# Second norm on ScalarE, one convolution tap and the sum on VectorE, and the norm shifts on POOL in the fuse phase of a ViT, memory and MoE kernel on one Trainium2 core

## The chip, the cores and the metric

One core of one Trainium2 chip runs the whole program in one launch. The metric is the time of the program on the device in microseconds (us). "Engines" are TensorE (PE in the rows, its weight loads PEld), VectorE (DVE), ScalarE (ACT), GpSimd (POOL) and SyncE (SP, which here only issues DMAs).

## The reference, cut to what matters

The model is a small vision transformer over 64 images (196 patches and a class token, 128 wide, 4 layers), then a memory block over 197 + 32 text tokens for each image, then a mixture of experts. The changed phase stands between the transformer and the memory block. It computes this:

```python
h = layernorm(h, norm_w, norm_b)                   # first norm: last step of the transformer
h = jnp.concatenate([h, txt], axis=1)              # 197 + 32 = 229 tokens
z = _layernorm(h)                                  # second norm: (h - mean) / sqrt(var + eps)
xc = conv1d_depthwise(z, conv_w, taps=4, padding=(3, 0)) + conv_b[:, None]
eta_mean   = sigmoid(xc + gelu(xc @ eta_w1) @ eta_w2).mean(axis=(0, 2))
alpha_mean = sigmoid(xc + gelu(xc @ alpha_w1) @ alpha_w2).mean(axis=(0, 2))
```

Each output token of the convolution is, channel by channel, a weighted sum of its own token and the three before it; tap 3 is the token's own. `xc` is kept for the memory block, and the two means become the decay and the drift of the memory.

## The kernel before

The program is a row of phases with a barrier behind each: `layers_phase` (the transformer), `fuse_phase` (the changed one), `gate_phase` (means and scans), `memory_phase` and `tail_phase` (routing and experts). `fuse_phase` works on pairs of images: 32 pairs, 458 tokens each (`WL`). A pair lies as four tiles of 99 or 98 tokens (token on the partition, 128 channels along the row) and a fifth with the 2 x 32 text tokens.

Each engine runs its own loop over an index `i`, unrolled, in the order in which its code is written, and does a different stage of a different pair in each pass: a software pipeline. Semaphores (`f_...`) tie the engines, and an engine does not go past a wait. The stages of pair `n` are, in this order:

- First norm, for pairs from 6 on (the first six were normed in the layers phase): `first_stats` and `first_aggr` (mean and variance into `mv`), `first_rstd` on POOL (`ve` = variance + eps, then `rstd` by a power of -0.5), `first_shift` on VectorE (-mean x rstd), `normalise` on ScalarE (x * rstd + shift into `y`), `weight` on VectorE and `bias` on POOL. SP then writes `y` to memory as `hcat`.
- Second norm: `second_stats` and `second_aggr` on VectorE, `second_rstd` on POOL, `scale` on VectorE: `z` = y x rstd. The mean is not taken off here. Instead the four diagonal matrices of the convolution are multiplied once, ahead of the loop, by (identity - 1/128), into `diag`.
- `turn` on TensorE: five transposes into the bank `f_T`, with the image tokens of both images first and the text tokens behind them. `turned_out` on ScalarE copies the bank into `zT` in two instructions, so that each image's 229 tokens stand in a row behind three zero columns.
- `conv` on TensorE: four matmuls, one for each tap, added up in the bank `f_C`. `conv_out` on ScalarE adds the bias and writes `xc`, a slice of `xT`.
- `up` on TensorE, `gelu` on ScalarE, `down` on TensorE, `argument` on VectorE (adds `xc`), `tanh` on ScalarE (the sigmoid), `sums` on POOL: twice each, for eta and alpha.

Around the middle of the phase one pass of a loop does `down(i-2)`, `conv(i+1)`, `turn(i+2)`, `up(i)` on TensorE, and `sums(i-3)`, `second_rstd(i+4)`, `bias(i+5)`, `first_rstd(i+7)` on POOL. `memory_phase`, which the change leaves alone, has a norm whose steps are laid out as those of the changed kernel are: variance + eps and -mean on VectorE (L1573, L1574), power and shift on POOL (L1520, L1523).

Of the kernel before, what the change touches and what calls it, by code (L numbers as in the profile page):

```python
# [977 lines left out]
def fuse_phase(nc, g, A):  # L978

    LAST = 7  # L980
    with ExitStack() as ctx:
        s = Sems(nc, ctx, "f_taps f_gate_w f_txt f_set f_diag f_centred "
                 + " ".join(f"f_txt{p} f_out{p}" for p in range(4)) +
                 " f_stats f_aggr f_ve f_rstd f_shift f_xn f_xw f_y f_stats2 f_aggr2 f_ve2 f_rstd2 "
                 "f_z f_turned f_zT f_conv f_xc f_up f_gelu f_down f_arg f_tanh f_sum")

        def sb(name, shape, dt=F32):
# [5 lines left out]
        mv, ve, rstd, shift = ([sb(f"{n}{p}", [TC, 4, w]) for p in range(2)]
                               for n, w in (("mv", 2), ("ve", 1), ("rstd", 1), ("shift", 1)))
        mv2, ve2 = sb("mv2", [TC, 5, 2]), sb("ve2", [TC, 5, 1])
        rstd2 = [sb(f"rstd2{p}", [TC, 5, 1]) for p in range(2)]
# [18 lines left out]
        with nc.Block() as block:  # L1015
# [1192 lines left out]
```

## Time and profile before

| what | value |
|---|---|
| median of 3 runs | 3659.69 us (3652.66 to 3664.78) |
| the profiled execution's own time | 3660.88 us |
| its span | 3659.1 us |
| mean granted TensorE clock | 0.975 of full speed |
| fuse phase, first instruction to barrier | about 2600 to 2850 us of the span |
| busy over the span | PE 3379.4, DVE 2384.5, POOL 2279.2, ACT 2018.8 us |

The whole program is listed by engine in the profile, but the changed phase is only 7% of it. So the busy shares of the span say little here, and the rows further down come from views that are cut to that phase: busy time by stretch, instructions in order of time, and the minimum, median and maximum duration of one line's instructions.

### The profile page before, as it was taken

What the parts mean: (1) busy time and instruction counts of PE and PEld (TensorE: products, weight loads), DVE (VectorE), ACT (ScalarE), POOL (GpSimd) and SP (SyncE); (2) the same over time, 40 slices, a digit from 0 to 9 for tenths busy, and PEclk for the clock granted to TensorE, in tenths of its full rate; (3) what the DMA queues carried; (4) which work ended last, traced back from release to release, by engine and by line L of the source; (5) the groups of instructions that cost most, each with busy time, mean ns of one, the idle gap of its engine ahead of it and who ended that gap; (6) DMA issues with size and microseconds to landing.
All of it is one profiled execution on the core that took longest, in us unless ns stands there. A gap on an engine that the chain in (4) does not pass through costs nothing. (4 is left out here: it accounts for less than half of the span.)

```text
span 3659.1 us, 87958 instructions
## 1 busy us (share of the span) xinstructions
PE 3379.4 (92%) x29756; PEld 2580.2 (71%) x29756; DVE 2384.5 (65%) x6229; ACT 2018.8 (55%) x3948; POOL 2279.2 (62%) x2634
## 2 busy tenths in 40 slices
PE   7999999989999899999999999999899898999983
PEld 4577787777787677777777777777544686766762
DVE  2267777657777666777766677766698677885110
ACT  0156666656666665666665666667465464323331
POOL 0356664576666386666548666637598684377886
PEclk9999999999999999999999999999999899999997
DMA  6856675046766315766703666640111133143443
GB/s 221 271 110 127 127 132 104 9 84 127 132 129 127 60 28 105 129 127 127 131 12 61 123 128 127 130 82 1 39 33 27 54 83 58 35 105 74 68 62 32
DMA packets 456073, 342.26 MB, mean 94 GB/s; under 512 B 70659, under 2 KB 440171, under 8 KB 455595
## 3 DMA queue, kind: packets, MB, share of 16 engines
q1 hardware_dynamic: 404419, 275.69, 38.9%
q10 hardware_dynamic: 24224, 46.44, 3.9%
q0 software_dynamic: 27136, 16.42, 3.4%
q8 instruction: 159, 2.61, 0.3%
q14 instruction: 135, 1.11, 0.1%
HBM read 227.68 MB, written 109.29 MB: 92 GB/s over the span
## 5 line engine op out<-in xcount | busy, mean ns | idle before, releaser
L795 DVE TENSOR_REDUCE a_neg_max<-a_S 99x4 f32<-99x788 f32 x1024 | 1003.7, 980 | 484.9 <-PE a_S L346 481.3
L558 ACT ACTIVATE a_shared<-a_St 99x792 f32<-99x792 f32 (+1 forms) x1024 | 851.2, 831 | 637.2 <-PE a_St L363 626.0
L363 PE MATMUL a_St<-a_q_st,a_k_st 99*99 99x198 bf16 (+1 forms) x4096 | 527.8, 251 | 55.4 <-DMA a_q_st<-a_max_rows 39.1
L346 PE MATMUL a_S<-a_k_st,a_q_st 96*99 96x197 bf16 x4096 | 538.7, 254 | 39.4 <-DVE a_neg_max L795 39.4
L346 PEld LDWEIGHTS a_S<-a_k_st,a_q_st 96*99 96x99 bf16 x4096 | 390.0, 126 | 255.0 <-DVE a_neg_max L795 216.8
L382 PE MATMUL a_O<-a_shared,a_v_aug 99*32 99x198 f32 (+1 forms) x8192 | 464.8, 339 | 0.4
L363 PEld LDWEIGHTS a_St<-a_q_st,a_k_st 99*99 99x99 bf16 (+1 forms) x4096 | 390.3, 126 | 84.9 <-DMA a_q_st<-a_max_rows 48.1
L707 POOL CAST a_parts<-a_q_k 128x792 bf16<-128x792 f32 x128 | 107.8, 842 | 321.3 <-issue 281.2
L382 PEld LDWEIGHTS a_O<-a_shared,a_v_aug 99*32 99x32 f32 (+1 forms) x8192 | 247.0, 110 | 84.3 <-issue 1.8
L687 POOL CAST a_max_parts<-a_neg_max 99x32 bf16<-99x32 f32 x128 | 26.8, 210 | 406.7 <-DVE a_neg_max L795 406.7
L498 PEld LDWEIGHTS a_O<-a_w,a_shared 128*99 128x99 f32 x2048 | 243.2, 167 | 40.8 <-issue 23.1
L498 PE MATMUL a_O<-a_w,a_shared 128*99 128x128 f32 x2048 | 265.6, 273 | 0.9 <-DVE h L892 0.9
L1934 POOL DMA_INDIRECT out<-h,token x128 | 210.1, 1641 | 53.7 <-issue 36.3
L627 ACT ACTIVATE a_shared<-a_St,a_cols 128x396 f32<-128x396 f32 x256 | 148.7, 590 | 152.1 <-PE a_St L509 144.5
L709 POOL TENSOR_TENSOR a_q_k<-a_q_k,a_parts 128x792 f32<-128x792 f32 x128 | 216.2, 1689 | 10.3
L715 POOL TENSOR_TENSOR a_parts<-a_q_k,a_parts 128x792 bf16<-128x792 f32 x128 | 215.7, 1685 | 10.3
L509 PE MATMUL a_St<-a_shared,a_w 128*128 128x396 f32 x512 | 196.2, 506 | 0.0
L723 POOL TENSOR_TENSOR h<-h,a_rows 99x512 f32<-99x512 f32 x128 | 162.9, 1273 | 34.8 <-ACT a_shared L634 34.8
L1878 ACT ACTIVATE z_gel<-z_U,z_sb 128x458 f32<-128x458 f32 x128 | 81.9, 644 | 174.0 <-PE z_U L1756 165.1
L1878 ACT ACTIVATE z_gel<-z_U,z_eb 128x458 f32<-128x458 f32 x128 | 82.4, 644 | 165.0 <-PE z_U L1756 153.2
L1981 DVE TENSOR_TENSOR h<-z_O,xT 120x512 f32<-120x512 f32 x32 | 22.1, 690 | 225.3 <-DMA out<-h,token 176.6
L634 ACT ACTIVATE a_shared<-h,a_m_rstd 99x128 f32<-99x128 f32 x512 | 162.1, 390 | 3.2 <-POOL a_m_rstd L734 3.2
(271 smaller groups left out, 7312.4 us busy)
## 6 DMA issues: line engine op xcount, KB each, us to landing
a_shared<-in_x ACTq DMA_DIRECT2D x64, 594.0 KB, 5.0
spill_q<-a_parts SPq DMA_DIRECT2D x384, 99.0 KB
spill_k<-a_parts SPq DMA_DIRECT2D x384, 99.0 KB
a_k_st<-spill_k SPq DMA_DIRECT2D x128, 297.0 KB, 4.0
a_q_st<-spill_q SPq DMA_DIRECT2D x128, 297.0 KB, 6.2
a_k_st<-spill_k SPq DMA_DIRECT2D x128, 198.0 KB, 4.6
a_q_st<-spill_q SPq DMA_DIRECT2D x128, 198.0 KB, 6.7
a_k_st<-spill_k SPq DMA_DIRECT2D x128, 99.0 KB, 4.9
```

What stands on the lines that cost most here:

```text
L346: mm = nc.tensor.matmul(S[0:TC, j // 2, j % 2 * TB:j % 2 * TB + NTOK], q_st[p % 4][0:SPLIT, head, b * TB + c * TC:b * TB + (c + 1) * TC], ...
L363: mm = nc.tensor.matmul(St[0:keys, j // 2, j % 2 * TB:(j % 2 + 1) * TB], k_st[p][:, head, first:first + keys], q_st[p][:, head, b * TB:(b ...
L382: mm = nc.tensor.matmul(O[32 * j:32 * j + 32, half * TB:(half + 1) * TB], v_aug[p % 4][0:keys, 2 * b + c, half * 4 + j, :], probs[0:keys, ...
L498: mm = nc.tensor.matmul(O[0:TC, t * D:(t + 1) * D], gl[k % 2][:, h, t * TC:(t + 1) * TC], m.w2[:, h * D:(h + 1) * D], start=(h == 0), stop ...
L509: nc.tensor.matmul(St[:, h, 0:PW], m.w1[:, h * 128:(h + 1) * 128], m_yT[n % 2], start=True, stop=True).then_inc(s["m_fc1"], 1)
L558: nc.scalar.activation(probs[0:keys, u % 4, :].rearrange("p (x t) -> p x t", x=2), St[0:keys, :, 0:2 * TB], ACT.Exp).then_inc(s["probs"], 1)
L709: nc.gpsimd.tensor_tensor(q_k[:], q_k[:], parts[:, 0, :, :], ALU.subtract).then_inc(s["res"], 1)
L715: nc.gpsimd.tensor_tensor(parts[:, 2, :, :], q_k[:], parts[:, 1, :, :], ALU.subtract).then_inc(s["lo"], 1)
L723: nc.gpsimd.tensor_tensor(hp, hp, m.b2.unsqueeze(1).to_broadcast([TC, 4, D]), ALU.add).then_inc(s["m_bias"], 1)
L795: nc.vector.tensor_reduce(out.rearrange("p (x y) -> p x y", x=2), S[0:TC, :, 0:2 * TB].rearrange("p x (y t) -> p x y t", y=2)[:, :, :, 0:N ...
L1878: nc.scalar.activation(gel[n % 2][:, k, 0:WL], U[k][:, 0:WL], ACT.Gelu_apprx_tanh, bias=bias).then_inc(s["gelu"], 1)
L1934: nc.gpsimd.indirect_dma_start(out=out[:, :], out_offset=bass.IndirectOffsetOnAxis(g.token[0:n, e, k:k + 1].bitcast(U32), 0), in_=y[(2 * e ...
```

## The change

Five parts, all in `fuse_phase`:

1. ScalarE computes the second norm in full: `normalise_again` makes `z` = y x rstd + shift, in five instructions of 99 x 128, as `normalise` does for the first norm. VectorE's `scale` goes, and so do the matmul and the copy that centred the diagonal matrices.
2. Both shifts are made on POOL, behind the power (-mean x rstd, 99 x 4 or 99 x 5). The small additions of eps, until now on POOL, and the -mean are done by VectorE right behind each `bn_aggr`, on tiles of 4 or 5 columns. VectorE's `first_shift` goes.
3. The convolution keeps taps 0 to 2 on TensorE. Tap 3 with the bias is `first_part` on VectorE: it reads the turned rows in PSUM and writes `xc`. `conv_sum` on VectorE adds the bank `f_C` to it. ScalarE's `conv_out` goes, and `turn` waits for `first_part` too.
4. `turn` writes the text rows to their final place (its fifth transpose writes 2 x 32 columns), so that ScalarE's `turned_out` is one copy of 458 columns.
5. The order of the loops differs: on ScalarE `gelu`, `normalise`, `tanh`, `normalise_again`, `turned_out`; on VectorE `first_part` leads and `conv_sum` ends, with both `argument` in the middle; on POOL `first_rstd` is moved from the end of a pass, for pair i+7, to the head of the next pass, for pair i+6.

```diff
                 def conv(n):
...
-                    for k in range(4):
+                    for k in range(3):
...
                 def turn(n):
                     wait(pe, s["f_z"], n + 1)
                     wait(pe, s["f_zT"], n)
+                    wait(pe, s["f_first"], n)
...
-                def conv_out(n):
-                    wait(act, s["f_conv"], n + 1)
-                    nc.scalar.activation(xc(n), Cp[:, 0:WL], ACT.Identity, bias=taps[:, 4:5]).then_inc(s["f_xc"], 1)
+                def normalise_again(n):
+                    wait(act, s["f_shift2"], n + 1)
+                    wait(act, s["f_turned"], n - 1)
+                    for t in range(5):
+                        a = nc.scalar.activation(z[n % 2][:, t, :], normed(n, t), ACT.Identity,
+                                                 bias=shift2[n % 2][:, t, :], scale=rstd2[n % 2][:, t, :])
+                    a.then_inc(s["f_z"], 1)
...
-                    nc.scalar.activation(zT[n % 2][:, :, 3:3 + NTOK],
-                                         Tp[:, 0:2 * NTOK].rearrange("p (b l) -> p b l", b=2), ACT.Copy)
-                    nc.scalar.activation(zT[n % 2][:, :, 3 + NTOK:],
-                                         Tp[:, 2 * NTOK:WL].rearrange("p (b l) -> p b l", b=2),
+                    nc.scalar.activation(zT[n % 2][:, :, 3:], Tp[:, 0:WL].rearrange("p (b l) -> p b l", b=2),
                                          ACT.Copy).then_inc(s["f_zT"], 1)
...
                 def second_rstd(n):
-                    wait(pool, s["f_aggr2"], n + 1)
-                    wait(pool, s["f_rstd2"], n)
-                    nc.gpsimd.tensor_tensor(ve2[:, :, 0], mv2[:, :, 1], g.eps[0:TC, 0:1].to_broadcast([TC, 5]),
-                                            ALU.add).then_inc(s["f_ve2"], 1)
-                    wait(pool, s["f_ve2"], n + 1)
+                    wait(pool, s["f_ve2"], 2 * (n + 1))
                     wait(pool, s["f_z"], n - 1)
-                    nc.gpsimd.tensor_tensor(rstd2[n % 2][:, :, 0], ve2[:, :, 0],
+                    nc.gpsimd.tensor_tensor(rstd2[n % 2][:, :, 0], ve2[n % 2][:, :, 0],
                                             g.neg_half[0:TC, 0:1].to_broadcast([TC, 5]),
                                             ALU.pow).then_inc(s["f_rstd2"], 1)
+                    wait(pool, s["f_rstd2"], n + 1)
+                    nc.gpsimd.tensor_tensor(shift2[n % 2][:, :, 0], nm2[n % 2][:, :, 0], rstd2[n % 2][:, :, 0],
+                                            ALU.mult).then_inc(s["f_shift2"], 1)
...
-                def scale(n):
-                    wait(dve, s["f_rstd2"], n + 1)
-                    wait(dve, s["f_turned"], n - 1)
...
+                def first_part(n):
...
+                    wait(dve, s["f_zT"], n + 1)
+                    nc.vector.tensor_scalar(xc(n), Tp[:, 0:WL], taps[:, 3:4], taps[:, 4:5], ALU.mult,
+                                            ALU.add).then_inc(s["f_first"], 1)
+
+                def conv_sum(n):
+                    wait(dve, s["f_conv"], n + 1)
+                    wait(dve, s["f_first"], n + 1)
+                    nc.vector.tensor_tensor(xc(n), Cp[:, 0:WL], xc(n), ALU.add).then_inc(s["f_xc"], 1)
...
                 def second_aggr(n):
...
+                    wait(dve, s["f_aggr2"], n + 1)
+                    wait(dve, s["f_shift2"], n - 1)
+                    nc.vector.tensor_scalar(ve2[n % 2][:, :, 0], mv2[:, :, 1], EPS, None, ALU.add).then_inc(s["f_ve2"], 1)
+                    nc.vector.tensor_scalar(nm2[n % 2][:, :, 0], mv2[:, :, 0], -1.0, None, ALU.mult).then_inc(s["f_ve2"], 1)
```

The first norm's `first_rstd` and `first_aggr` are changed as the second norm's are, with 4 columns for 5.

On VectorE, one pass of the middle of the phase is these rows in the kernel before (`f_z<-f_y` is `scale`, `f_shift` is `first_shift`, `f_arg` is `argument`, `f_mv` is one of the two `bn_aggr`):

```order
L1199 TENSOR_TENSOR f_z<-f_y,f_rstd 99x640
L1210 BN_STATS f_stats<-f_y 99x6 x5
L1230 SCALAR_TENSOR_TENSOR f_shift<-f_mv,f_rstd 99x4
L1236 BN_STATS f_stats<-h 99x6 x4
L1217 BN_AGGR f_mv<-f_stats 99x2 x5
L1222 TENSOR_TENSOR f_y<-f_y,norm 99x512
L1249 TENSOR_TENSOR f_arg<-f_Z,xT 128x458
L1243 BN_AGGR f_mv<-f_stats 99x2 x4
L1249 TENSOR_TENSOR f_arg<-f_Z,xT 128x458
```

and these in the changed one:

```order
L1191 TENSOR_SCALAR xT<-f_T,f_taps 128x458
L1206 BN_STATS f_stats<-f_y 99x6 x5
L1213 BN_AGGR f_mv<-f_stats 99x2 x5
L1217 TENSOR_SCALAR f_ve<-f_mv 99x5
L1218 TENSOR_SCALAR f_nm<-f_mv 99x5
L1247 TENSOR_TENSOR f_arg<-f_Z,xT 128x458 x2
L1222 TENSOR_TENSOR f_y<-f_y,norm 99x512
L1229 BN_STATS f_stats<-h 99x6 x4
L1237 BN_AGGR f_mv<-f_stats 99x2 x4
L1241 TENSOR_SCALAR f_ve<-f_mv 99x4
L1242 TENSOR_SCALAR f_nm<-f_mv 99x4
L1197 TENSOR_TENSOR xT<-f_C,xT 128x458
```

The two instructions with two inputs in SBUF that led to `z` and to the shift are out; two that read PSUM and four of 4 or 5 columns are in, and each `bn_aggr` now stands right behind its statistics. On POOL, one pass was this (`gate_sum` is `sums`):

```order
L1146 TENSOR_TENSOR gate_sum<-gate_sum,f_arg 128x458 x2
L1152 TENSOR_TENSOR f_ve<-f_mv,eps 99x5
L1156 TENSOR_TENSOR f_rstd<-f_ve,neg_half 99x5
L1162 TENSOR_TENSOR f_y<-f_y,norm 99x512
L1170 TENSOR_TENSOR f_ve<-f_mv,eps 99x4
L1174 TENSOR_TENSOR f_rstd<-f_ve,neg_half 99x4
```

and is now this:

```order
L1166 TENSOR_TENSOR f_rstd<-f_ve,neg_half 99x4
L1170 TENSOR_TENSOR f_shift<-f_nm,f_rstd 99x4
L1143 TENSOR_TENSOR gate_sum<-gate_sum,f_arg 128x458 x2
L1149 TENSOR_TENSOR f_rstd<-f_ve,neg_half 99x5
L1153 TENSOR_TENSOR f_shift<-f_nm,f_rstd 99x5
L1158 TENSOR_TENSOR f_y<-f_y,norm 99x512
```

The two additions of eps are gone from POOL, a product stands behind each power, and the first norm's power leads the pass.

## Rows read from the trace of the kernel before

**Rows 1.** Busy us (xcount) of PE, PEld, DVE, ACT, POOL in a stretch; PEclk.

```profile
2640.00:2740.00 100.00, 99.34 (x297) 48.34 (x295) 97.04 (x317) 62.56 (x153) 93.76 (x97) 1.00 0.13 34
```

**Rows 2.** `conv_out` by itself in three stretches: count, first to last start.

```profile
L1109 ACT ACTIVATE xT<-f_C,f_taps x7: 622/642/644, 2619.8 to 2659.9; 128x458 f32<-128x458 f32 x7
...
L1109 ACT ACTIVATE xT<-f_C,f_taps x21: 619/623/625, 2659.9 to 2805.1; 128x458 f32<-128x458 f32 x21
...
L1109 ACT ACTIVATE xT<-f_C,f_taps x6: 625/642/643, 2805.1 to 2838.6; 128x458 f32<-128x458 f32 x6
```

**Rows 3.** Timeline, middle of the phase: start, us, engine, line, [idle before].

```profile
2741.19 1.27 POOL L1162 TENSOR_TENSOR f_y<-f_y,norm 99x512 f32<-99x512 f32 x1
2741.25 1.88 DVE L1199 TENSOR_TENSOR f_z<-f_y,f_rstd 99x640 f32<-99x640 f32 x1
...
2743.06 1.05 DVE L1210 BATCH_NORM_STATS2 f_stats<-f_y 99x6 f32<-99x128 f32 x5
...
2744.27 2.10 POOL L1146 TENSOR_TENSOR gate_sum<-gate_sum,f_arg 128x458 f32<-128x458 f32 x2
2744.33 1.13 DVE L1230 SCALAR_TENSOR_TENSOR f_shift<-f_mv,f_rstd 99x4 f32<-99x4 f32 x1 [0.21 <-POOL f_rstd L1174]
...
2745.50 1.65 ACT L1103 ACTIVATE f_y<-h,f_shift,f_rstd 99x128 f32<-99x128 f32 x4 [2.73 <-DVE f_shift L1230]
...
2746.16 0.42 DVE L1217 BATCH_NORM_AGGREGATE f_mv<-f_stats 99x2 f32<-99x6 f32 x5
...
2747.08 0.62 DVE L1249 TENSOR_TENSOR f_arg<-f_Z,xT 128x458 f32<-128x458 f32 x1
...
2747.82 0.30 PEld L1046 LDWEIGHTS f_Z<-f_gel,f_gate_w 128*128 128x128 f32 x2 [0.79 <-issue]
```

**Rows 4.** Timeline, end of the phase: PE's weight loads at `down` and `conv`.

```profile
2819.61 0.19 PEld L1046 LDWEIGHTS f_Z<-f_gel,f_gate_w 128*128 128x128 f32 x1 [0.19 <-issue]
...
2826.51 0.19 PEld L1046 LDWEIGHTS f_Z<-f_gel,f_gate_w 128*128 128x128 f32 x1 [0.19 <-issue]
...
2830.35 0.19 PEld L1055 LDWEIGHTS f_C<-f_zT,f_diag 128*128 128x128 f32 x1 [0.20 <-issue]
2830.73 0.19 PEld L1055 LDWEIGHTS f_C<-f_zT,f_diag 128*128 128x128 f32 x1 [0.20 <-issue]
```

**Rows 5.** Single lines: duration in ns, minimum/median/maximum.

```profile
L1230 DVE SCALAR_TENSOR_TENSOR f_shift<-f_mv,f_rstd x26: 139/1132/1137, 2625.7 to 2802.4; 99x4 f32<-99x4 f32 x26
...
L1156 POOL TENSOR_TENSOR f_rstd<-f_ve,neg_half x32: 1164/1176/1285, 2610.3 to 2818.5; 99x5 f32<-99x5 f32 x32
```

**Rows 6.** Timeline of the memory phase, where the same small steps stand already.

```profile
2886.38 1.27 POOL L1506 TENSOR_TENSOR y_hc<-y_hc,y_qn 115x512 f32<-115x512 f32 x1
...
2886.89 0.79 DVE L1573 TENSOR_SCALAR y_ve<-y_mv 115x4 f32<-115x4 f32 x1
...
2955.82 0.55 ACT L1478 ACTIVATE xT<-y_ZT 128x458 f32<-128x458 f32 x1
2955.88 0.17 DVE L1573 TENSOR_SCALAR y_ve<-y_mv 115x4 f32<-115x4 f32 x1
2955.95 0.16 DVE L1574 TENSOR_SCALAR y_nm<-y_mv 115x4 f32<-115x4 f32 x1
...
2956.20 1.02 POOL L1520 TENSOR_TENSOR y_rstd<-y_ve,neg_half 115x4 f32<-115x4 f32 x1 [0.81 <-DVE y_nm L1574]
...
2957.29 0.20 POOL L1523 TENSOR_TENSOR y_shift<-y_nm,y_rstd 115x4 f32<-115x4 f32 x1
```

**Rows 7.** Timeline, start of the phase: a power on POOL beside VectorE.

```profile
2624.13 1.35 POOL L1174 TENSOR_TENSOR f_rstd<-f_ve,neg_half 99x4 f32<-99x4 f32 x1
...
2624.52 0.29 DVE L1199 TENSOR_TENSOR f_z<-f_y,f_rstd 99x128 f32<-99x128 f32 x1
```

**Rows 8.** Timeline, late in the phase: `scale` beside `sums`.

```profile
2806.34 3.96 DVE L1199 TENSOR_TENSOR f_z<-f_y,f_rstd 99x640 f32<-99x640 f32 x1 [0.26 <-POOL f_rstd L1156]
...
2807.51 2.10 POOL L1146 TENSOR_TENSOR gate_sum<-gate_sum,f_arg 128x458 f32<-128x458 f32 x2
```

More of the change, by code:

```diff
@@ L990, in fuse_phase @@
         taps, gate_w, norm = sb("taps", [D, 5]), sb("gate_w", [D, 4, D]), g.norm
-        centre, tap_diag, diag = sb("centre", [D, D]), sb("tap_diag", [D, 4, D]), sb("diag", [D, 4, D])
+        diag = sb("diag", [D, 3, D])
         stats, stats2 = sb("stats", [TC, 4, 6]), sb("stats2", [TC, 5, 6])
[L993 to L996, printed above, removed]
+        mv, mv2 = sb("mv", [TC, 4, 2]), sb("mv2", [TC, 5, 2])
+        ve, nm, rstd, shift = ([sb(f"{n}{p}", [TC, 4, 1]) for p in range(2)] for n in ("ve", "nm", "rstd", "shift"))
+        ve2, nm2, rstd2, shift2 = ([sb(f"{n}2{p}", [TC, 5, 1]) for p in range(2)] for n in ("ve", "nm", "rstd", "shift"))
         y = [sb(f"y{p}", [TC, 5, D]) for p in range(4)]
@@ L1132, in _ @@
                         normalise(i + 6)
-                    if live(i + 1):
-                        conv_out(i + 1)
+                    if live(i - 2):
+                        tanh(i - 2)
+                    if live(i + 3):
+                        normalise_again(i + 3)
                     if live(i + 2):
                         turned_out(i + 2)
-                    if live(i - 2):
-                        tanh(i - 2)
             @block.gpsimd
@@ L1167, in first_rstd @@
                     p = n % 2
-                    wait(pool, s["f_aggr"], n + 1 - NORMED)
-                    wait(pool, s["f_rstd"], n - 1 - NORMED)
-                    nc.gpsimd.tensor_tensor(ve[p][:, :, 0], mv[p][:, :, 1], g.eps[0:TC, 0:1].to_broadcast([TC, 4]),
-                                            ALU.add).then_inc(s["f_ve"], 1)
-                    wait(pool, s["f_ve"], n + 1 - NORMED)
+                    wait(pool, s["f_ve"], 2 * (n + 1 - NORMED))
                     wait(pool, s["f_xn"], n - 1 - NORMED)
@@ L1176, in first_rstd @@
                                             ALU.pow).then_inc(s["f_rstd"], 1)
+                    wait(pool, s["f_rstd"], n + 1 - NORMED)
+                    nc.gpsimd.tensor_tensor(shift[p][:, :, 0], nm[p][:, :, 0], rstd[p][:, :, 0],
+                                            ALU.mult).then_inc(s["f_shift"], 1)
                 nc.gpsimd.memset(g.gate_sum[:], 0.0).then_inc(s["f_set"], 1)
@@ L1256, in _ @@
                     if i == 4 - LAST:
[L1257 removed]
                         dve.wait_ge(s["f_taps"], 16)
[L1259 to L1260 removed]
+                        for k in range(3):
+                            nc.vector.tensor_scalar(diag[:, k, :], g.ident[:], taps[:, k:k + 1], None,
                                                     ALU.mult).then_inc(s["f_diag"], 1)
[L1262 to L1266 removed]
+                    if live(i + 1):
+                        first_part(i + 1)
                     if live(i + 4):
                         second_stats(i + 4)
[L1269 to L1270 removed]
+                        second_aggr(i + 4)
+                    if live(i - 2):
+                        argument(i - 2, 0)
+                        argument(i - 2, 1)
+                    if NORMED <= i + 5 < PAIRS:
+                        weight(i + 5)
                     if NORMED <= i + 7 < PAIRS:
                         first_stats(i + 7)
[L1273 to L1279 removed]
                         first_aggr(i + 7)
[L1281 to L1282 removed]
+                    if live(i + 1):
+                        conv_sum(i + 1)
         s.clear()
```

71 lines of the change are left out of this document (21 added, 50 removed).

## The prediction

> **What bounds the kernel now.** The changed phase is 7% of the span, so I cut every view to it. Busy time by stretch [rows 1]: in 100 us of its middle PE is busy 99.3, VectorE 97.0, POOL 93.8 and ScalarE 62.6 us. Three engines look full, so the shares don't say which one paces.
>
> Pitch first [rows 2]: `conv_out` runs once for each pair. The first 7 starts span 40.1 us (6 gaps, 6.68 each), the next 20 gaps 145.2 us (7.26 each), the last 5 gaps 33.5 us (6.70).
>
> Does PE need 7.26? At the end of the phase, with the first norm over, its loads at `down` stand 2826.51 - 2819.61 = 6.90 us apart, with no more than the usual 0.19 us ahead of them [rows 4]. In the middle there is 0.79 us of idle ahead of the same load at 2747.82, which comes 0.12 us after VectorE's `argument` (L1249, 2747.08 + 0.62) has emptied the bank that `down` writes [rows 3]. The profile calls that idle "issue", but by the code it is that wait. So VectorE paces, with PE 0.36 us behind it.
>
> Why does VectorE need 7.26? Two of its instructions are far too long. `first_shift` (L1230, 4 columns) takes 0.139 us at best and 1.132 in the median [rows 5]. In the timeline it starts 0.06 us after `sums` on POOL and ends with the first of the two (2.10 us for both) [rows 3]. `scale` (L1199) takes 1.88 us; it starts 0.06 us behind POOL's `bias`, which takes 1.27 us [rows 3]. Once it took 3.96 us, with `sums` started after it (at 2807.51, 2.10 us) ahead of its end [rows 8]. So a VectorE instruction with its inputs in SBUF doesn't run beside a long one of POOL: about 1.0 us lost in the shift and 1.1 in `scale`, for each pair.
>
> **The change part by part**, in us for each pair of the middle.
>
> PE: a tap is two passes, and passes are 0.38 apart [rows 4], so -0.77. PE's own need: 6.90 - 0.77 = 6.13. The transposes have the same sizes.
>
> VectorE: out go `scale` (1.81 to the next start) and the shift (its 0.21 of waiting and 1.05 to the next start) [rows 3]: -3.07. In come two passes over 458 columns out of PSUM. The nearest row is `argument`, 0.62 long [rows 3], which costs about 0.56 as each starts some 0.06 to 0.08 ahead of the last one's end: +1.12. A one-source read of PSUM of that size isn't in these rows; the bounds are 0.55 (ScalarE's copy of the size [rows 6]) and 0.62, and I take 0.56. In come four small ones, 0.07 each from start to start [rows 6]: +0.28. Each `bn_aggr` now waits for its own statistics, and the small ones for it: four times some 0.1, the lost overlap and 0.04 of handing over: +0.4. Sum: 7.26 - 3.07 + 1.12 + 0.28 + 0.4 = 6.0, without waits for POOL.
>
> ScalarE: four normalising instructions take 1.65 [rows 3], 0.39 each; five are +1.95. `conv_out` (0.62) goes. The two copies of the turned rows become one of 0.55, by a copy of the same size [rows 6]. With 62.6 / 100 x 7.26 = 4.54 busy before, that is about 4.54 + 1.95 - 0.6 = 5.9: below PE.
>
> POOL: the additions of eps go; two products of 0.20 come [rows 6]. Its pass is now: power of 4 columns with the product's start 1.09 behind it [rows 6], product 0.16, `sums` 2.10 [rows 3], power of 5 columns 1.18 [rows 5] + 0.07, product 0.16, `bias` 1.25 [rows 3]. Sum 6.0.
>
> No engine alone needs more than PE's 6.13, so what links them decides. The link that I find is a ring between POOL and VectorE. POOL's second power needs `nm2`. VectorE's small pair is single-source, but it also waits for POOL: L1573, 4 columns, took 0.79 instead of 0.17 and ended (2887.68) with POOL's L1506 (2886.38 + 1.27 = 2887.65) [rows 6]. So the pair goes through when `sums` end, and POOL, idle meanwhile, starts its power 2956.20 - 2955.88 = 0.32 after the pair's start [rows 6]. The same happens at the other pair: `weight`, then `bias` on POOL 1.25 long, meanwhile statistics and `bn_aggr` on VectorE (about 1.3), then the pair when `bias` ends, and again 0.32. The ring is 6.0 + 0.32 + 0.32 = 6.65. Between them `weight` (512 columns, taken as 0.57 of holding, as `argument` costs 0.56 with 458) can hold up POOL's product by 0 to 0.57: it starts 0.14 + 1.12 = 1.26 behind the pair and ends at 1.83, and the product is due at 0.32 + 1.25 = 1.57, so 0.26. That gives 6.65 to 7.2 as bounds, 6.91 by this arithmetic; I take **6.85**, as the second hand-over can partly hide behind `bias`.
>
> A second ring: `first_part` 0.56, statistics 1.05 + 0.04, `bn_aggr` 0.42 + 0.04, the small pair 0.14, two `argument` 0.56 + 0.62, then ScalarE: `tanh` about 0.55, `normalise_again` 1.95, the copy 0.55 and 0.05 of handing over, after which `first_part` of the next pair may start: 6.5 [rows 3, 6]. It is shorter than the first, so it doesn't pace.
>
> Must POOL's powers be counted among the long holders? By the trace not: L1174 is on POOL from 2624.13 for 1.35 us, and L1199 on VectorE, both inputs in SBUF, starts at 2624.52 inside it and takes 0.29 us [rows 7]. The power computes long on 4 numbers and holds nothing. *The Trainium skill (SBUF — State Buffer, section SBUF: two separate sides) states of the read ports that GpSimd and VectorE share that whichever starts first "gets the pair for the whole instruction; the other fully blocks". The trace agrees for `first_shift` and `scale` [rows 5, 8]. Taken to the letter it makes the powers holders too; the power's row speaks against that, and my sum goes by them.*
>
> In total. 20 gaps: 20 x (7.26 - 6.85) = -8.2. The last 5, where the first norm runs out and PE paces: -0.77 for about three of them and -0.3 for two: -2.9. The first 6: they are paced by the long way of each early pair over all engines. `conv_out` ahead of the copy on ScalarE is gone from it and a tap; -3, against +1 to +2 for the first pair, whose `z` now takes 1.95 on ScalarE after a product, where VectorE needed about one. With the matmul and copy of the centring gone, which the first `conv` waited for: net -2.5. Behind the last `conv`: one tap, -0.8. Sum -14.4. Later phases do the same work from a barrier. From the profiled time 3660.9: 3646.5. That execution was 1.2 above the median of its runs, so 3645.3, **3645 us**, for the median.
>
> The granted clock is 1.00 in the middle [rows 1]. PE would still be busy in 9 tenths of a pass, and I count no change of it.
>
> **The rivals.**
>
> *The second ring paces* (6.5): if `weight` misses the product and the pairs meet POOL between two instructions, the first ring falls to PE's and ScalarE's. 20 x 0.75 = -15, and -6 at the ends: 3639. For it: [rows 6], where the pair passes in 0.17 at 2955.88. Against: POOL has little idle time in which to be met.
>
> *The powers hold the ports too.* `weight` would then be asked for at 1.26 behind the pair, with the second power on POOL until 1.57: 0.2 to 0.3 more for each pair, 20 x 0.2 = +4, so 3649. Against: [rows 7]. The page's sentence above is this rival's.
>
> *The waits come back.* VectorE still needs SBUF at three points of a pass (two small pairs, `weight`), and POOL holds it 3.4 of 7 us. If these cost 1.25 together where I count 0.6, the ring is 7.2 to 7.3, and only the ends gain their 6: 3652 to 3655, no change that 3 runs can tell. For it: [rows 8], a VectorE instruction that stood behind POOL for longer than the 2.1 of both `sums`. Against: in the new order POOL's next instruction behind `sums` and behind `bias` waits for the pair itself, so it can't slip in.
>
> *Slower.* The small pair of the second norm is ready during the first of the `sums` and loses to the second too, as `scale` did in [rows 8]. It then waits up to 2.1, and the two `argument`, `tanh`, `normalise_again` and the copy, queued behind it in the second ring, all move: 6.5 + 2.1 = 8.6 at most, say 8.2. 20 x 0.95 = +19, less 6 at the ends: 3673. It turns the gain into a loss from a ring of 7.57 on, that is from 1.05 of waiting there, one whole `sums` instruction, and shows as slower from 8.1. Against it: the first power starts only when `nm` is done, `sums` end 3.35 later, and the pair asks about 0.8 + 2.1 after `nm`, within the second one.
>
> **How the numbers follow.** What a measurement can tell from no change is 0.3%, 11 us: faster is below 3648.7, slower above 3670.7. Forecast 0.44 (3641 to 3650), powers as holders 0.04, second ring 0.22, waits come back 0.22, slower 0.08. To "same" go 0.04 of the forecast, the powers and the waits whole, and 0.01 of the slow one: faster 0.40 + 0.22 = 0.62, same 0.31, slower 0.07. The range that leaves out 2 in 10 is 3634 to 3657: from PE pacing at 6.13 to 6.3 at the low end, to the returned waits at the high one.
>
> **What would show it.** After: a pitch of `conv_sum` of 6.85 in 20 gaps; no 0.79 us ahead of `down` but a wait of PE ahead of `conv` or `turn`; the small instructions of the second norm long (0.2 to 0.5) and ending with `sums`, those of the first norm with `bias`; POOL busy nearly all the time, with two idle spots of 0.2 to 0.3 released by `nm`. A pitch of 6.5 with POOL idle waiting for VectorE or ScalarE shows the second ring; `f_ve` near 1 us or above, the waits. The forecast is wrong if the small instructions don't ask for what POOL holds, if an instruction out of PSUM does, or if the way of the first pairs grows more than I count.

## The result and the profile after

| | kernel before | changed kernel |
|---|---|---|
| median (range), 10 runs each on one chip | 3652.73 us (3647.07 to 3664.78) | 3637.41 us (3625.36 to 3645.24) |
| ratio of the two, 95% interval | | 0.9944, 0.9929 to 0.9959 |
| time of the profiled execution | 3660.88 us | 3640.64 us |
| its span, mean granted clock | 3659.1 us, 0.975 | 3638.8 us, 0.974 |
| fuse phase in it | 249.7 us | 231.8 us |

The change gained 0.56% by the ratio of the comparison, 15.3 us (0.42%) between the medians and 20.2 us between the two profiled executions. The median of before over ten runs is 7 us below that of its first three, so the forecast is better read by its difference, 14.4 us less, than by its 3645 us. Here and below the phase is the time from the first instruction of `fuse_phase` (POOL's memset of `gate_sum`) to the first of the next phase (VectorE's memset of `g_ones`). It lost 17.9 us; the other 2.3 us lie in phases that are the same in both kernels.

The same view as [rows 2], now of `conv_sum`, which writes `xc` where `conv_out` did: count, duration in ns (minimum/median/maximum), first to last start.

```profile
L1197 DVE TENSOR_TENSOR xT<-f_C,xT x7: 623/625/635, 2619.0 to 2656.5; 128x458 f32<-128x458 f32 x7
L1197 DVE TENSOR_TENSOR xT<-f_C,xT x21: 623/627/635, 2656.5 to 2788.8; 128x458 f32<-128x458 f32 x21
L1197 DVE TENSOR_TENSOR xT<-f_C,xT x6: 623/630/635, 2788.8 to 2819.3; 128x458 f32<-128x458 f32 x6
```

| stretch of the phase | before | after | difference | forecast |
|---|---|---|---|---|
| its start to the first `xc` | 19.0 | 19.7 | +0.7 | in the next row |
| first 6 gaps | 40.1 | 37.5 | -2.6 | -2.5 for both rows |
| next 20 gaps | 145.2 | 132.3 | -12.9 | -8.2 |
| last 5 gaps | 33.5 | 30.5 | -3.0 | -2.9 |
| from the last `xc` to the end | 11.9 | 11.8 | -0.1 | -0.8 |
| phase | 249.7 | 231.8 | -17.9 | -14.4 |

So the middle gained 4.7 us more than forecast and the ends together 1.2 less (5.0 where 6.2 was forecast). In the middle the regular gap is 6.69 us, where 6.85 was forecast, and one gap, when the statistics of the first norm run out, is 5.23 (before it is 5.45 and falls into the next stretch).

Busy time in the middle, the view of [rows 1] (PE, PEld, DVE, ACT, POOL, then PEclk):

```profile
2640.00:2740.00 100.00, 95.60 (x286) 46.05 (x285) 91.94 (x404) 88.31 (x210) 91.65 (x105) 1.00 0.14 36
```

All four engines are now near 90%, and none is full. What holds them shows in the order of time. The timeline of the changed kernel, one pass of the middle (start, us, engine, line, [idle before it and what ended it]):

```profile
2703.48 1.02 POOL L1166 TENSOR_TENSOR f_rstd<-f_ve,neg_half 99x4 f32<-99x4 f32 x1 [0.20 <-DVE f_nm L1242]
2704.34 0.75 DVE L1191 TENSOR_SCALAR xT<-f_T,f_taps 128x458 f32<-128x458 f32 x1 [0.41 <-ACT f_zT L1115]
2704.36 2.57 PE L1054 MATMUL f_C<-f_zT,f_diag 128*128 128x458 f32 x6 [0.30 <-ACT f_zT L1115]
2704.57 0.20 POOL L1170 TENSOR_TENSOR f_shift<-f_nm,f_rstd 99x4 f32<-99x4 f32 x1
2704.73 2.11 POOL L1143 TENSOR_TENSOR gate_sum<-gate_sum,f_arg 128x458 f32<-128x458 f32 x2
2705.01 1.05 DVE L1206 BATCH_NORM_STATS2 f_stats<-f_y 99x6 f32<-99x128 f32 x5
2706.10 0.45 DVE L1213 BATCH_NORM_AGGREGATE f_mv<-f_stats 99x2 f32<-99x6 f32 x5
2706.58 0.28 DVE L1217 TENSOR_SCALAR f_ve<-f_mv 99x5 f32<-99x5 f32 x1
2706.78 0.16 DVE L1218 TENSOR_SCALAR f_nm<-f_mv 99x5 f32<-99x5 f32 x1
2706.85 1.16 DVE L1247 TENSOR_TENSOR f_arg<-f_Z,xT 128x458 f32<-128x458 f32 x2
2707.02 1.18 POOL L1149 TENSOR_TENSOR f_rstd<-f_ve,neg_half 99x5 f32<-99x5 f32 x1 [0.18 <-DVE f_nm L1218]
2707.51 1.13 ACT L1121 ACTIVATE f_arg<-f_arg 128x458 f32<-128x458 f32 x2 [0.79 <-DVE f_arg L1247]
2707.94 0.68 DVE L1222 TENSOR_TENSOR f_y<-f_y,norm 99x512 f32<-99x512 f32 x1
2708.27 0.40 POOL L1153 TENSOR_TENSOR f_shift<-f_nm,f_rstd 99x5 f32<-99x5 f32 x1
2708.54 0.86 DVE L1229 BATCH_NORM_STATS2 f_stats<-h 99x6 f32<-99x128 f32 x4
2708.54 2.02 ACT L1108 ACTIVATE f_z<-f_y,f_shift,f_rstd 99x128 f32<-99x128 f32 x5
2708.69 1.27 POOL L1158 TENSOR_TENSOR f_y<-f_y,norm 99x512 f32<-99x512 f32 x1
2709.43 0.38 DVE L1237 BATCH_NORM_AGGREGATE f_mv<-f_stats 99x2 f32<-99x6 f32 x4
2709.84 0.17 DVE L1241 TENSOR_SCALAR f_ve<-f_mv 99x4 f32<-99x4 f32 x1
2709.92 0.16 DVE L1242 TENSOR_SCALAR f_nm<-f_mv 99x4 f32<-99x4 f32 x1
2710.16 1.02 POOL L1166 TENSOR_TENSOR f_rstd<-f_ve,neg_half 99x4 f32<-99x4 f32 x1 [0.20 <-DVE f_nm L1242]
2710.47 0.53 ACT L1115 ACTIVATE f_zT<-f_T 128x458 f32<-128x458 f32 x1
...
2711.03 0.75 DVE L1191 TENSOR_SCALAR xT<-f_T,f_taps 128x458 f32<-128x458 f32 x1 [0.40 <-ACT f_zT L1115]
```

Two rings of equal length can be read off, start to start.

- **Ring 1, POOL and VectorE**: power of 4 columns 1.09, product 0.16, `sums` 2.11, wait 0.18, power of 5 columns 1.25, product 0.42, `bias` 1.27, wait 0.20: 6.68. Inside it, `f_ve` (L1217) starts at 2706.58 and ends with `sums` (2704.73 + 2.11 = 2706.84), and the product (L1153) takes 0.40 in place of 0.20, as `weight` (L1222) runs till 2708.62. POOL's row adds up to the pitch in any case, as its waits are in the sum. Read back from what ends the second wait, the ring leaves POOL when `sums` end and runs over VectorE: the rest of the pair, both `argument`, `weight`, statistics, `bn_aggr` and the pair of 4 columns stand there one behind the other, and POOL's power starts 3.32 after the end of `sums`. POOL's own way over that stretch (0.18, 1.25, 0.42, 1.27) is done after 3.12.
- **Ring 2, VectorE and ScalarE**: `first_part` 0.67, statistics 1.09, `bn_aggr` 0.48, the small pair 0.27, `argument` 0.66 until ScalarE's `tanh`, both `tanh` 1.03, `normalise_again` 1.93, the copy (2710.47) and its hand-over 0.56 until the next `first_part` (2711.03): 6.69. VectorE waits 0.41 at its end for the copy. But 0.12 of it is `f_ve`'s wait for `sums`; free of that wait it would be 6.57.

So ring 2 borrows its last 0.12 from ring 1, or the other way round. Equal lengths don't tell which sets the pace; the experiments do.

### The profile page after: what moved, and what is told of

Read it like the earlier page. It is cut to its first block and busy times, and to the rows that moved or that the text cites. A ratio compares the mean times of both kernels' runs of the same rounds, so it can differ in the third digit from the quotient of the medians.

```text
span 3638.8 us, 88045 instructions
## 1 busy us (share of the span) xinstructions
PE 3358.6 (92%) x29690; PEld 2572.5 (71%) x29690; DVE 2363.4 (65%) x6342; ACT 2063.2 (57%) x4044; POOL 2263.2 (62%) x2634
## 5 line engine op out<-in xcount | busy, mean ns | idle before, releaser
L346 PEld LDWEIGHTS a_S<-a_k_st,a_q_st 96*99 96x99 bf16 x4096 | 390.1, 126 | 256.3 <-DVE a_neg_max L795 219.1
L723 POOL TENSOR_TENSOR h<-h,a_rows 99x512 f32<-99x512 f32 x128 | 163.1, 1274 | 33.5 <-ACT a_shared L634 33.5
```

What stands on the lines that cost most here:

```text
L346: mm = nc.tensor.matmul(S[0:TC, j // 2, j % 2 * TB:j % 2 * TB + NTOK], q_st[p % 4][0:SPLIT, head, b * TB + c * TC:b * TB + (c + 1) * TC], ...
L723: nc.gpsimd.tensor_tensor(hp, hp, m.b2.unsqueeze(1).to_broadcast([TC, 4, D]), ALU.add).then_inc(s["m_bias"], 1)
```

## The experiments

Every kernel was compared with the kernel before on its own chip, where that had a median of 3698.79 us (e1 to e4), 3657.38 us (e5 to e8) and 3655.34 us (one run, e9 to e11). Ratios compare across chips, times don't; the phase of the changed kernel was 231.8 and 232.3 us on two chips (e8). The pitch, the gap between two pairs, is read from the timeline and repeats to 0.02 us within a kernel, apart from one pair that comes 0.3 late in some kernels and makes it up. The phase as a whole varies by 2 us more, since VectorE waits at its start for the text tokens' transfer (5.7 us in the changed kernel, 8.4 in e7), so that the first `xc` comes 19.0 to 22.2 us after the start. Where that matters, the time from the first `xc` to the end of the phase is given too: 230.7 before, 212.1 in the changed kernel (211.7 in e8).

### e1: the small pair reads PSUM

```diff
-        mv, mv2 = sb("mv", [TC, 4, 2]), sb("mv2", [TC, 5, 2])
+        mv = sb("mv", [TC, 4, 2])
+        mv2 = ctx.enter_context(nc.psum_tensor("f_mv2", [128, 512], F32))[0:TC, 0:10].rearrange(...)
```

> The changed kernel with one edit: the second norm's mean and variance (mv2) lie in PSUM, so that VectorE's small pair f_ve, f_nm reads no SBUF. The changed kernel has a pitch of 6.69 us a pair, with f_ve at 0.28 us where it takes 0.17 alone. Theory A (two rings locked together: the pair is let through when POOL's sums end, and this sets POOL's and VectorE's pass): the pair no longer waits, f_ve falls to 0.2 or less, and what is left is the ring over VectorE and ScalarE without its 0.12 us: pitch 6.55 to 6.60, phase 2 to 3 us shorter than the changed kernel's. Rival B (the ring over VectorE and ScalarE alone paces): the same here, 6.57. Rival C (POOL and VectorE alone pace, through the hand-over before the second power): f_ve shorter, but POOL starts its power as early as sums end, pitch down by 0.1 to 0.2. Rival D (f_ve's 0.28 is no port wait): no change of f_ve, pitch 6.69.

Ratio 0.9946 (0.9927 to 0.9966), phase 230.9 (from the first `xc` 209.6), pitch 6.58. The rows of `f_ve`, of POOL and of `weight` in e1:

```profile
L1218 DVE TENSOR_SCALAR f_ve<-f_mv x20: 164/165/166, 2657.8 to 2782.8; 99x5 f32<-99x5 f32 x20
```

```profile
2702.00 2.11 POOL L1144 TENSOR_TENSOR gate_sum<-gate_sum,f_arg 128x458 f32<-128x458 f32 x2
2704.18 1.18 POOL L1150 TENSOR_TENSOR f_rstd<-f_ve,neg_half 99x5 f32<-99x5 f32 x1
2705.10 0.68 DVE L1223 TENSOR_TENSOR f_y<-f_y,norm 99x512 f32<-99x512 f32 x1
2705.44 0.40 POOL L1154 TENSOR_TENSOR f_shift<-f_nm,f_rstd 99x5 f32<-99x5 f32 x1
```

With its input in PSUM the pair no longer waits, and POOL goes from `sums` to the power with 0.07 between them. The pitch fell only to ring 2's 6.57. VectorE still waits 0.41 for the copy. Only rival D falls by this: theory A and rivals B and C all allowed what came.

### e2: ScalarE copies the turned rows first

```diff
-                    if live(i + 3):
-                        normalise_again(i + 3)
                     if live(i + 2):
                         turned_out(i + 2)
+                    if live(i + 3):
+                        normalise_again(i + 3)
```

> The changed kernel with one edit: on ScalarE turned_out stands ahead of normalise_again, so that the five normalising instructions (1.95 us) are out of the ring VectorE first_part, statistics, arguments, ScalarE tanh, copy. Rival B (that ring alone paces): pitch falls from 6.69 to about 6.15 to 6.3, phase 10 us shorter. Theory A (the ring over POOL, closed by the pair that waits for the end of sums, is just as long): pitch stays within 0.1 of 6.69, first_part no longer waits for ScalarE, and f_ve waits longer for POOL instead (0.6 to 1.0 us where it was 0.28). The start may gain 0.7 us.

Ratio 0.9934 (0.9914 to 0.9954), phase 231.0 (from the first `xc` 209.9), pitch 6.68. Rival B is out: it had the pitch at 6.3 or less. Ring 2 is cut open, and VectorE doesn't wait at `first_part` any more. It waits at the pair instead, 0.49 longer than in the changed kernel:

```profile
L1217 DVE TENSOR_SCALAR f_ve<-f_mv x20: 481/777/786, 2660.2 to 2785.9; 99x5 f32<-99x5 f32 x20
```

### e3: both

The edits of e1 and e2 together.

> Both edits together (mv2 in PSUM, and turned_out ahead of normalise_again). Theory A: only both together open the two rings, pitch 6.15 to 6.3, close to TensorE's own 6.12; phase 10 to 12 us shorter than the changed kernel's, time 3624 to 3628 where the changed kernel has 3637. Rival B: the same as the copy alone. Rival C: the same as the pair alone.

Ratio 0.9915 (0.9894 to 0.9935), phase 219.1 (from the first `xc` 198.8), pitch 6.17. Neither edit alone moved the phase by more than 1 us, both together took 12.7 us out of it. From the first `xc` on, e1 gained 2.5 us (0.11 for each pair of the middle) and e2 2.2 (at the end of the phase, nothing in the middle), hidden in the phase by a later start; together they gained 13.3. Both rivals, with the pitch of one edit alone (6.68 or 6.58), are out. POOL and `weight` in e3:

```profile
2699.06 1.18 POOL L1150 TENSOR_TENSOR f_rstd<-f_ve,neg_half 99x5 f32<-99x5 f32 x1
2699.58 0.68 DVE L1223 TENSOR_TENSOR f_y<-f_y,norm 99x512 f32<-99x512 f32 x1
2700.32 0.20 POOL L1154 TENSOR_TENSOR f_shift<-f_nm,f_rstd 99x5 f32<-99x5 f32 x1
...
2705.23 1.18 POOL L1150 TENSOR_TENSOR f_rstd<-f_ve,neg_half 99x5 f32<-99x5 f32 x1
```

The product is back to 0.20: `weight` starts 0.52 into the power and is over (2700.26) before the product is due. The pair in PSUM alone doesn't do that: in e1 ring 2 holds VectorE back, `weight` starts 0.92 into the power, and the product takes 0.40. The middle stretch is 121.9 us, and VectorE has no gap left in a pass. Here the pair of the first norm does wait for `bias`, as the prediction had it: its `f_ve` takes 0.27 (2701.49 to 2701.77, `bias` ends at 2701.74).

### e4: four taps on PE again

The convolution as before (four taps on PE, `conv_out` on ScalarE, now ahead of `tanh`), norms and shifts as changed.

```diff
-                    for k in range(3):
+                    for k in range(4):
...
+                    if live(i + 1):
+                        conv_out(i + 1)
                     if live(i - 2):
                         tanh(i - 2)
...
-                    if live(i + 1):
-                        first_part(i + 1)
...
-                    if live(i + 1):
-                        conv_sum(i + 1)
```

> The changed kernel with part 3 undone: four taps on TensorE, the bias by ScalarE's conv_out as before, neither first_part nor conv_sum on VectorE; the rest of the change stays. Theory A: VectorE is lighter by 1.2 us, TensorE needs 6.89 again and paces: pitch 6.90, so the change without this part gains about 20 x 0.36 = 7 us in the phase's middle instead of 12. Rival (the third part brings nothing, since VectorE and not TensorE holds the pass): pitch 6.7 or below.

Ratio 1.0029 (1.0015 to 1.0043), phase 258.6, pitch 7.38: slower than the kernel before. The pitch of 6.90 that PE would set was missed, and so was the rival's 6.7. ScalarE's timeline in e4:

```profile
2705.81 0.64 ACT L1105 ACTIVATE xT<-f_C,f_taps 128x458 f32<-128x458 f32 x1 [1.02 <-PE f_C L1054]
2706.35 1.05 ACT L1124 ACTIVATE f_arg<-f_arg 128x458 f32<-128x458 f32 x2
2707.30 2.02 ACT L1111 ACTIVATE f_z<-f_y,f_shift,f_rstd 99x128 f32<-99x128 f32 x5
2709.22 0.53 ACT L1118 ACTIVATE f_zT<-f_T 128x458 f32<-128x458 f32 x1
```

It reads as a ring of ScalarE and PE: `conv` starts at 2702.43, `conv_out` 3.38 later, then 0.54, 0.95, 1.92 to the copy and 0.59 to the next `conv`: 7.38. The long `normalise_again` is queued between `conv_out` and the copy that the next `conv` needs.

### e5: e4 with the copy first

The swap of e2, in e4's kernel.

> The kernel of e4 (four taps on PE, conv_out on ScalarE, the rest as changed) with one more edit: ScalarE does turned_out ahead of normalise_again. Its pitch in e4 was 7.38 and the phase 258.6. Theory: e4 was paced by a ring of PE and ScalarE alone, conv 3.38, conv_out 0.54, both tanh 1.05, normalise_again 1.95 and the copy 0.55, because the copy stands behind normalise_again. With the copy ahead of it the ring is 5.5 and PE's own need of 6.90 paces: pitch 6.9, phase 258.6 - 20 x 0.48 = 249, about the kernel before, ratio 0.999 to 1.001. Rival: e4 was paced by VectorE's argument waiting for down and by the small pair waiting for POOL, which the swap leaves or makes worse: pitch 7.2 to 7.4, phase 255 to 259, ratio 1.002 to 1.003.

Ratio 0.9958 (0.9939 to 0.9976), phase 242.2. The pitch is 6.90, as the theory had it. The ratio is better than the expected 0.999 to 1.001 and the phase 7 us shorter than expected, since the ends were paced by e4's ring too: 9.7 us came from the middle, 4.4 from the first six gaps and 1.9 from the last five. Weight loads of e5, one pass apart and with no gap but the usual one:

```profile
2700.14 0.19 PEld L1054 LDWEIGHTS f_C<-f_zT,f_diag 128*128 128x128 f32 x1 [0.20 <-issue]
...
2707.04 0.19 PEld L1054 LDWEIGHTS f_C<-f_zT,f_diag 128*128 128x128 f32 x1 [0.19 <-issue]
```

So PE's need with four taps is 6.90, as [rows 4] had it. Against e2, which differs from e5 in the convolution alone, the moved tap is worth 11.2 us of phase (242.2 - 231.0); in the changed kernel's order (e4 against e8) it is worth 26.3.

e5 also shows what the prediction's slower rival is made of. Both instructions of the pair wait, each for one of the two `sums`:

```profile
2698.19 2.11 POOL L1149 TENSOR_TENSOR gate_sum<-gate_sum,f_arg 128x458 f32<-128x458 f32 x2
2698.38 1.00 DVE L1223 TENSOR_SCALAR f_ve<-f_mv 99x5 f32<-99x5 f32 x1
2699.29 1.03 DVE L1224 TENSOR_SCALAR f_nm<-f_mv 99x5 f32<-99x5 f32 x1
```

That is 1.7 us of waiting for each pair (0.17 and 0.16 are the durations without it). It costs nothing here, as PE paces.

### e6: both small pairs read PSUM

```diff
-        mv = sb("mv", [TC, 4, 2])
+        mv = ctx.enter_context(nc.psum_tensor("f_mv", [128, 512], F32))[0:TC, 0:8].rearrange(...)
```

> The kernel of e3 (mv2 in PSUM, copy first; pitch 6.18, phase 219.1) with the first norm's mv in PSUM too. Its f_ve of 4 columns takes 0.26 in e3, as it waits for the rest of bias; here 0.17, and the first f_nm follows 0.1 earlier. If VectorE paces e3 (its instructions stand one behind the other over all 6.18), the pitch falls by 0.1 to 6.08 and the phase by 2 to 217. If PE paces it, as its row of loads without a gap beyond the usual ones says, nothing changes: phase 219, plus or minus 1.

Ratio 0.9882 (0.9857 to 0.9906), phase 219.7. Both halves of the expectation came in part. In the middle the pitch of `conv_sum` is 6.08, VectorE's own; PE, with loads 6.12 apart (2699.61 and 2705.73) and no gap but the usual one, falls behind, and the last five gaps are 6.13 each where e3 has shorter ones. From the seventh `xc` to the last it is 151.7 us, in e3 151.3. So PE's three taps are the floor, and the phase is e3's. The phase doesn't explain the lower ratio; the intervals of the two overlap.

### e7: two copies again

```diff
-                    nc.scalar.activation(zT[n % 2][:, :, 3:], Tp[:, 0:WL]...
+                    nc.scalar.activation(zT[n % 2][:, :, 3:3 + NTOK], rows_T[:, :, 0:NTOK], ACT.Copy)
+                    nc.scalar.activation(zT[n % 2][:, :, 3 + NTOK:], rows_T[:, :, NTOK:],
```

> The changed kernel with turned_out as two instructions again (394 and 64 columns), all else as changed (pitch 6.69, phase 231.8). Theory: a ring of VectorE and ScalarE runs through this copy, so its length counts in full until the small pair meets POOL between two instructions: the ring was 6.57 without the pair's wait. Two copies cost about 0.2 more than one: ring 6.77, pitch 6.75 to 6.85, phase 233 to 235, ratio against the kernel before 0.001 above that of the changed one. Rival: POOL alone paces (6.0 of work and hand-overs), and ScalarE's extra 0.2 is idle time used: phase 231 to 232.

Ratio 0.9932 (0.9912 to 0.9952), phase 234.1, of which 22.2 lie ahead of the first `xc` (after: 19.7). The middle is 132.2 us, as in the changed kernel (132.3): the expected 0.06 to 0.16 for each pair did not come, and from the first `xc` on it is 211.9, as without the edit. But the pair's wait shrank, from 0.284 to 0.226:

```profile
L1219 DVE TENSOR_SCALAR f_ve<-f_mv x20: 170/226/237, 2660.5 to 2787.4; 99x5 f32<-99x5 f32 x20
```

Two copies cost 0.06 more than one by that, not 0.2, and ring 2 took it out of its slack. That was the first sign that ring 1 sets the pace alone.

### e8: the changed kernel again

> The changed kernel, unaltered, on the chip of the other three, so that their times can be set against it directly: ratio 0.9944 (0.9929 to 0.9959), phase 231.8 plus or minus 1. A phase more than 1 us off would say that differences of 1 us between profiles mean nothing.

Ratio 0.9938 (0.9921 to 0.9956), phase 232.3, middle 132.2 us.

### e9, e10, e11: one ring made longer, then the other, then both

e9 adds a small product on POOL, e10 a small copy on ScalarE ahead of `turned_out`, each into a tile that nobody reads; e11 has both.

```diff
+                    nc.gpsimd.tensor_tensor(more[:, :, 0], nm[p][:, :, 0], rstd[p][:, :, 0], ALU.mult)
...
+                    nc.scalar.activation(more[:], taps[:, 0:4], ACT.Copy)
```

> The changed kernel (pitch 6.69 in the middle, phase 231.8 and 232.3 in two profiles) with one more small product on POOL for each pair, of 99 x 4, into a tile that nobody reads, ahead of the first norm's shift. Small products of POOL start 0.15 ahead of the next instruction. Theory: a ring of POOL and VectorE sets 6.69, and the ring of VectorE and ScalarE, 6.57 to 6.6 by itself, follows behind. Then the 0.15 counts in full: pitch 6.84, phase 235. Rival: VectorE and ScalarE pace and POOL's gaps of 0.18 and 0.20 ahead of its powers are spare time that takes it up: pitch 6.69, phase 232.

> The changed kernel with one more small instruction on ScalarE for each pair, a copy of 128 x 4 into a tile that nobody reads, ahead of turned_out. No trace here has one of that size; bounds for its cost are 0.1 and 0.25. Theory: the ring through ScalarE is 6.62 with two copies and 6.57 with one, so it takes the lead from POOL's 6.69 as soon as more than 0.12 is added: pitch 6.57 + 0.1 to 0.25 = 6.69 to 6.82, with 0.2 6.77, the pair of the second norm then at 0.17 without a wait for the port. Rival: POOL's ring alone decides, ScalarE has idle time enough (it waits 0.8 ahead of tanh): pitch 6.69, f_ve unchanged.

> Both additions of e9 and e10 in one kernel. Theory: two rings side by side, the longer one decides: pitch is the larger of what e9 and e10 show, about 6.84. Rival: what looks like two rings is one that goes through both engines, so that both additions count: 6.69 + 0.15 + 0.08 to 0.2, 6.92 or more.

The row of `f_ve` in the changed kernel, in e9, e10 and e11, over the same window:

```profile
L1217 DVE TENSOR_SCALAR f_ve<-f_mv x20: 278/284/294, 2659.8 to 2786.8; 99x5 f32<-99x5 f32 x20
```

```profile
L1219 DVE TENSOR_SCALAR f_ve<-f_mv x20: 429/435/444, 2656.6 to 2786.5; 99x5 f32<-99x5 f32 x20
```

```profile
L1220 DVE TENSOR_SCALAR f_ve<-f_mv x20: 173/188/195, 2657.5 to 2784.6; 99x5 f32<-99x5 f32 x20
```

```profile
L1221 DVE TENSOR_SCALAR f_ve<-f_mv x20: 331/335/342, 2657.8 to 2787.6; 99x5 f32<-99x5 f32 x20
```

Each ran once: 3638.64, 3630.43 and 3641.74 us, the kernel before 3655.34, so the times carry no weight here. The phases are 234.8, 232.1 and 237.0 us, of which 19.6, 19.9 and 21.5 lie ahead of the first `xc`.

Divided by 19 gaps, the starts give a pitch of 6.68, 6.84, 6.69 and 6.83. POOL's 0.15 counts in full, ScalarE's addition not at all, and the two don't add up. The duration tells how much slack ring 2 has: it is 0.170 without a wait, so 0.114, 0.265, 0.018 and 0.165. Pitch less slack is ring 2's own length: 6.57 and 6.57 without the added copy, 6.67 and 6.67 with it, so that costs 0.10. e10 came within 0.02 of the point where ring 2 takes over, so of its expectation neither side came whole: the pitch stayed at 6.69, and `f_ve` did change.

## Why the prediction was right, and where not

The mechanism held in the main: waits behind POOL were the loss, and a ring of POOL and VectorE sets the pace of the middle. The step that failed is the length of that ring, in its two hand-overs: 0.32 us each were put down, and 0.18 and 0.20 were measured, so the pitch is 6.69 and not 6.85. The forecast's 14.4 us stand close to the 15.3 between the medians partly by luck. In the profiles the phase lost 17.9, with 4.7 more than forecast in the middle and 1.2 less at the ends.

- **The waits behind POOL as the loss in the kernel before**: right. `scale` and `first_shift` are gone, the pitch fell from 7.26 to 6.69, and the one VectorE instruction that still waits inside its row, `f_ve` of 5 columns, ends with POOL's `sums`.
- **Ring 1 sets the pace in the middle**: right. e9 and e11 show it, e7 and e10 show that ring 2 doesn't.
- **The way of its second half**: not as told. The prediction let the pair of the first norm wait for the end of `bias`. It doesn't: its `f_ve` (L1241) takes 0.170 in the changed kernel, e9 and e10 alike, and 0.161 with its input in PSUM (e6). By the rows of the changed kernel this half runs over VectorE's own instructions, 3.32 long, and POOL's way is 0.2 shorter. So whether the 0.26 that POOL's product waits for `weight` costs anything is not shown; e9 put its product into the first half, ahead of `sums`, and no run changed POOL's work in the second.
- **Its length, "6.85"**: this is the term that was mis-sized. The sum had 6.0 of POOL's own work and 0.26 of product waiting for `weight`; both are measured so (6.04 and 0.42 - 0.16 = 0.26). The two hand-overs were put at 0.32 each, from [rows 6], counted there from the pair's start with both its instructions still to run. Here `f_ve` of 5 columns has already started when POOL falls idle and ends within 0.05 of it, so only the rest of `f_nm` and a semaphore are left: 0.18. The second is 0.20. That takes 0.26 from the arithmetic's 6.91: 6.65, and start to start it is 6.68. The value taken, 6.85, was already 0.06 below that arithmetic, for a guess that the second hand-over would hide; it doesn't, it is as short as the first. 20 x 0.16 = 3.2 us of the 4.7 us miss come from there. The other 1.5 are the gap of 5.23 (6.69 - 5.23) that now falls into this stretch; the forecast had 20 equal gaps.
- **Ring 2, "6.5"**: nearly right, 6.57. It left out that `first_part` holds VectorE 0.67, not 0.56: it takes 0.75 us, above both bounds of the text (0.55 and 0.62).
- **PE's own need, 6.90 and 6.13**: right, by e5 (6.90) and e6 (6.12).
- **VectorE's own need, 6.0**: nearly right, 6.08 in e6.
- **The powers hold nothing**: right. `weight`, both inputs in SBUF, starts at 2707.94 inside L1149 (2707.02, 1.18 long) and takes 0.68, as it does throughout. *The Trainium skill (SBUF — State Buffer, section SBUF: two separate sides) says that whichever instruction starts first gets the shared ports for its whole length. The trace disagrees for the powers, and agrees for `sums`, which `f_ve` waits for, and for `weight`, which POOL's product waits for.*
- **The ends**: the last five gaps were right in sum (-3.0 for -2.9), though before's short gap of 5.45 is among them and after's is not. "Behind the last `conv`: one tap, -0.8" was a slip: that tap lies ahead of the last `xc`, in a gap that was already counted. Behind it there is -0.1. At the start, the first `xc` came 0.7 later, although VectorE's wait for the text tokens was 1.0 shorter than before (5.7 and 6.7). From the first statistics to the first `xc` the way of the first pair grew by 1.7 (11.6 to 13.3; 12.4 in e8), about the forecast's +1 to +2. The six gaps gave 2.6.
- **The signs named beforehand**: no 0.79 ahead of `down` but 0.30 ahead of `conv` came; `f_ve` of the second norm waits for `sums`, as forecast; that of the first norm was to wait for `bias` and doesn't. POOL's two idle spots ahead of its powers came, 0.18 and 0.20 long and not 0.2 to 0.3.

The right price of a hand-over stood in the trace of before, beside the row of L1573 at 2886.89 [rows 6] that the prediction took for the wait. POOL's L1506 ends at 2887.65, and the power starts 0.18 later, as in the changed kernel:

```profile
2887.59 0.16 DVE L1574 TENSOR_SCALAR y_nm<-y_mv 115x4 f32<-115x4 f32 x1
2887.83 1.02 POOL L1520 TENSOR_TENSOR y_rstd<-y_ve,neg_half 115x4 f32<-115x4 f32 x1 [0.18 <-DVE y_nm L1574]
```

*The Trainium skill (VectorE: DVE Perf Modes, section Mode 2×_2P — use both read ports for one tensor) says that the mode in which a one-source instruction takes both ports needs its data in SBUF. e1 agrees: with `mv2` in PSUM the same instruction takes 0.165 us beside `sums`, where it takes 0.284 in the changed kernel and 0.777 in e2.*

Part 3 of the change is worth more than PE's need tells, for a reason the prediction didn't give. By PE's 6.90 it would be 0.21 for each pair of the middle (6.90 - 6.69). It is 0.69 (7.38 in e4), and 26.3 us in the phase (e4 258.6, e8 232.3): with the second norm on ScalarE and the copy behind it, `conv_out` there closes a ring of 7.38. Either taking `conv_out` away (the change) or doing the copy first (e5) opens it.

What stays open: why e6 has a lower ratio than e3 at the same phase, the 2.3 us outside the phase, which no run here tells from chance, and whether less work for POOL behind `sums` would shorten the pitch of the changed kernel.

## What to carry to other kernels

When two engines take turns, write down every closed ring with its waits, not only each engine's sum. An engine's row, with its waits, always adds up to the pitch; what a ring is made of shows only when each wait is followed to the instruction that ends it. Two rings of nearly equal length hide each other: an edit that opens one gains little (2.5 us in e1, 2.2 in e2, from the first `xc` on) until the other is opened too (e3, 13.3 us). The duration of an instruction that waits inside its row, less its duration without a wait, is the slack of the shorter ring, readable to about 0.01 us. And price a hand-over from the moment at which the waited-for engine falls idle, not from the start of what it waits for.

## What the hardware showed beyond that

- A VectorE instruction of 99 x 5 waits for POOL when it reads SBUF and not when it reads PSUM: `f_ve` takes 0.777 in e2 and 0.165 in e3, and `f_nm` took 1.04 in e5. A spare bank for the small tile removes the wait.
- The waiting goes both ways: POOL's product of 99 x 5 takes 0.40 beside VectorE's `weight` and 0.20 without it (e3).
- `first_part` (one source in PSUM, two per-partition factors, 128 x 458) takes 0.754 us, `conv_sum` (PSUM and SBUF) of the same size 0.627.
- At the phase's start PE is granted 0.50 of its clock, the 1.2 GHz level, after 16 us without work, and the first `conv` takes 4.92 us for six passes; in the middle it is 2.57. The rows of the changed kernel, busy time by stretch and timeline:

```profile
2614.00:2618.00 4.00, 3.96 (x6) 1.87 (x7) 3.81 (x23) 1.82 (x5) 1.36 (x2) 0.50 0.38 97
```

```profile
2611.53 0.89 PE L1064 MATMUL f_T<-ident,f_z 99*128 99x99 f32 x4 [15.95 <-ACT f_z L1108]
2614.04 4.92 PE L1054 MATMUL f_C<-f_zT,f_diag 128*128 128x458 f32 x6 [1.32 <-ACT f_zT L1115]
```
